# The front of an attention and feed-forward kernel, written out block by block

## The chip, the cores and the metric

The kernel runs on one core of one Trainium2 chip, in one launch. The metric is the device time in microseconds (us), taken as the median of several executions. One further execution was profiled, and all rows below are of that one.

## The reference

x is 2 x 2048 tokens of 256 numbers, in float32.

```python
xn = layernorm(x)                                  # no gain, no bias
q, k, v = split(xn @ w_qkv)                        # 16 heads of 16
q, k = irfft(rfft(q) * mask), irfft(rfft(k) * mask)   # along each head's 16; mask = sigmoid(logits)
attn = softmax(q @ k.T / 4) @ v @ w_out + b_out
h = square(relu(xn @ W_fc.T)); y = h @ W_proj.T
spikes = 5 steps of a leaky integrate-and-fire on y, averaged
out = x + attn + spikes
```

The filter on q and k is linear in a head's 16 numbers, so the kernel folds it into the weights.

## The kernel before

The five engines have instruction streams of their own, written by hand: PE (matmul), DVE, ACT, POOL and SP, which issues the DMAs. Semaphores order them. The change concerns the front, the work before the first softmax, and leaves the 32 passes (16 heads x 2 batches) and the end as they are.

The front handles the 4096 tokens in 8 blocks of 512. x_in holds two blocks of x, x_norm two normalised ones. For a block t:

- SP loads x (`load_x`), 512 KB.
- DVE `normalise`: statistics (4 instructions and 4 aggregations), five small instructions for the root with one square root on ACT (`deviation`), and scaling (4 instructions).
- PE `transpose_block`: 8 transposes into `even_slot`; ACT `take_transposed` copies them to xb, POOL from there to xnT.
- PE `project_qk`: four groups w = 0 to 3, two for Q and two for K, each of 2 matmuls (4 instructions in the trace), into two PSUM banks in turn. ACT `take_high` copies a group to the high part of the buffer hilo[w], DVE `low_parts` subtracts it from the group for the low part and frees the bank: group w waits for the low part of group w - 2.
- SP `store_block`: two stores of 256 KB per group, from hilo[w] to the scratch qk_scratch in DRAM. hilo[w] lies in probs (w = 0, 1), relu_sb (2) and hid_sb (3). ACT writes hilo[w] of the next block only when these stores have landed (semaphore stored[w]).
- PE `project_v`: 16 instructions into `odd_slot`; ACT `take_v` copies them out.

The order is: on PE Q/K(t), transposes(t+1), V(t); on DVE low parts(t), normalise(t+2); on SP the load of x(t+2), then the stores of t. Before block 0, DVE builds the filter, PE folds it into the weights in `odd_slot` (`fold_filter`), and ACT copies these out.

Heads need, per 128 queries, the maximum over all keys ahead of the exponentials. `first_max` computes 48 such pieces (128 queries x 512 keys) for head 0 in the front: one matmul on PE and one reduction on DVE each, with two places in PSUM. Its operands are the stack (`load_stack`), read back from the scratch at the start of block 4, once the stores of blocks 0 to 3 have landed. In blocks 5 to 7 the matmuls stand between those of Q/K (8 a block) and in blocks 6 and 7 also between those of V (8 a block); 8 more follow after block 7. `split_shift` on DVE turns the maxima of the first 1024 queries into rows of the stack, which SP writes (`store_shift`).

After the front PE computes scores, ACT takes exponentials into probs (all stores must have landed, as hilo[0] and hilo[1] lie there), and PE multiplies with V.

Of the kernel before, what the change touches and what calls it, by code (L numbers as in the profile page):

```python
# [17 lines left out]
P = 128  # L18
# [8 lines left out]
BLK = 512  # L27
# [14 lines left out]
AHEAD = [0, 4, 8, 8]  # L42
# [16 lines left out]
def build(nc, x, wqk, wv, wout, bout, logits, wfc, wproj, basis, eye, out):  # L59
    with ExitStack() as ctx:  # L60
# [44 lines left out]
        x_norm = attn[:, 2 * KT:4 * KT, :].rearrange("p (b k) d -> p b k d", b=2)  # L105
# [30 lines left out]

        def score_slot(g):
            return ring[:, (4 * (g // 2) + g % 2) % 3, :]
# [11 lines left out]
        const_in = sem("const_in")  # L150
        late_in = sem("late_in")
# [17 lines left out]
        stored = [sem(f"stored{i}") for i in range(QB)]  # L169
        v_ready = sem("v_ready")  # L170
        v_taken = sem("v_taken")
        stack_in = [sem(f"stack_in{i}") for i in range(2)]
# [50 lines left out]
        def _(sp):  # L223
# [17 lines left out]
            def store_block(t):  # L241

                for w in range(QB):
                    g = w % 2
                    sp.wait_ge(lo_done, QB * t + w + 1 + QK_BANKS)
                    for part in range(2):
                        dst = qk_dram[w // 2, g * 8:(g + 1) * 8, part, :, bass.ds(t * BLK, BLK)]
                        sp.dma_start(dst, hilo[w][:, part, :]).then_inc(stored[w], 16)  # L248
# [43 lines left out]
            for t in range(NB // 2, NB):  # L292
                if t < NB - 2:
                    next_x(t, t % 2)
                if t == NB // 2:
                    for w in range(QB):
                        sp.wait_ge(stored[w], 32 * (NB // 2 + 1))
                    sp.wait_ge(zero_out, 64)
                    load_stack(0, 0)
# [3 lines left out]
                store_block(t)  # L303

                if t == NB // 2:
                    sp.dma_start(wfc_sb[:], wfc.rearrange("(c p) e -> p c e", p=P)).then_inc(late_in, 16)
                if t == NB // 2 + 1:
                    sp.dma_start(wproj_sb[:], wproj.rearrange("(c p) e -> p c e", p=P)).then_inc(late_in, 16)
                if t == NB // 2 + 2:
                    sp.dma_start(wout_sb[:], wout.rearrange("(c p) e -> p c e", p=P)).then_inc(late_in, 16)  # L310
                    sp.dma_start(bout_sb[:], bout.partition_broadcast(P)).then_inc(late_in, 16)
            store_shift(0, 0, 0)
            for w in range(QB):
                sp.wait_ge(stored[w], 32 * (NB + 1))
# [47 lines left out]
        def _(pool):  # L362
# [18 lines left out]
            for w in range(QB):  # L381
                pool.sem_inc(stored[w], 32)
# [69 lines left out]
        def _(act):  # L452
# [14 lines left out]
            def take_high(t):  # L467
                for w in range(QB):
                    act.wait_ge(qk_ready, QB * t + w + 1)
                    act.wait_ge(stored[w], 32 * (t + 1))  # L470
                    act.activation(hilo[w][:, 0, :].bitcast(F32R), qk_psum(w), ACT.Copy).then_inc(hi_ready, 1)
# [7 lines left out]
            take_transposed(0, 0)  # L479

# [4 lines left out]
            with act.Fori(0, NB // 4) as n:  # L485
                for p in range(2):
                    t = 2 * n + p
                    take_high(t)
                    take_transposed(t + 1, 1 - p)
                    deviation(t + 2)  # L490
                    take_v(t)
            for t in range(NB // 2, NB):
                take_high(t)
                if t < NB - 1:
                    take_transposed(t + 1, (t + 1) % 2)
                if t < NB - 2:
                    deviation(t + 2)
                take_v(t)
# [27 lines left out]
            for w in range(QB):  # L526
                act.wait_ge(stored[w], 32 * (NB + 1))
# [20 lines left out]
        def _(pe):  # L548
            def transpose_block(t, p):
                pe.wait_ge(ln_done, t + 1)  # L550
                for c in range(KC):
                    for k in range(KT):
                        mm = pe.transpose(even_slot[:, c * BLK + k * P:c * BLK + (k + 1) * P],
                                          x_norm[:, p, k, c * P:(c + 1) * P], ident[:])
                mm.then_inc(tr_done, 1)

            def fold_filter():

                pe.wait_ge(const_in, 48)
                pe.wait_ge(filt_dve, NF + 2)  # L560
                for w in range(QB):
# [6 lines left out]
            def first_max(n):  # L568

                tile, chunk, c = n // 4, n % 4, n % 2  # L570
                pe.wait_ge(mx_taken, n + 1)
                pe.matmul(mx[:, c, :], qst[0][:, tile * P:(tile + 1) * P], kst[0][:, chunk * BLK:(chunk + 1) * BLK],
                          start=True, stop=True).then_inc(mx_ready, 1)
# [31 lines left out]
            transpose_block(0, 0)  # L605
            fold_filter()
            pe.wait_ge(fold_taken, 1)
            with pe.Fori(0, NB // 4) as n:
                for p in range(2):
                    t = 2 * n + p  # L610
                    project_qk(t, p)
                    next_transpose(t + 1, 1 - p)
                    project_v(t, p)

            chunk = 0
            for t in range(NB // 2, NB):
                units = AHEAD[t - NB // 2]
                if units and not chunk:
                    pe.wait_ge(stack_in[0], STACK)
                    pe.wait_ge(blank_in, 16)  # L620
                    pe.wait_ge(preset, 8)
                project_qk(t, t % 2, chunk if units else None)
                if t < NB - 1:
                    next_transpose(t + 1, (t + 1) % 2)
                project_v(t, t % 2, chunk + 2 * QB if units > QB else None)
                chunk += 2 * units
# [32 lines left out]
            def pair(h, b, s, last=False, beside=lambda: None):  # L659
# [7 lines left out]
                if s == LEAD and ahead:  # L667
                    pe.wait_ge(stack_in[mb], STACK * (h + 1 + b))
# [48 lines left out]
            def head(h, b, last=False):  # L717
                i = 2 * h + b

                def beside(s):  # L720
# [5 lines left out]
                    if s == 10:  # L726
                        pe.wait_ge(misc_taken, use(i, DOWN))
                        pe.wait_ge(squared, 2 * i + 3)
                        down(0)
# [31 lines left out]
            pe.wait_ge(late_in, 64)  # L761
# [42 lines left out]

            end_transpose(0, 0)
# [11 lines left out]
        def _(dve):  # L817
            LN_LINKS = 7

            def normalise(t, n, p):  # L820

                base = LN_LINKS * t
                dve.wait_ge(x_landed[p], 16 * (n + 1))
# [10 lines left out]
                dve.tensor_scalar(rstd[:, 0, :], meanvar[:, :, 1], EPS, None, ALU.add).then_inc(var_ready, 1)  # L834
                dve.wait_ge(std_ready, t + 1)
# [9 lines left out]
                dve.wait_ge(ln_step, base + 7)  # L845
                dve.wait_ge(tr_done, t + 1)
                for k in range(KT):
                    last = dve.tensor_scalar(x_norm[:, p, k, :], x_in[:, p, k, :], meanvar[:, k, 0:1],
                                             rstd[:, 4, k:k + 1], ALU.subtract, ALU.mult)
                last.then_inc(ln_done, 1)  # L850

# [17 lines left out]
            def first_max(n):  # L869
                tile, chunk = n // 4, n % 4  # L870
# [10 lines left out]
            def low_parts(t, n=None):  # L881
                for w in range(QB):
                    if n is not None:
                        for c in range(2):
                            first_max(n + 2 * w + c)
                    dve.wait_ge(hi_ready, QB * t + w + 1)
                    dve.tensor_tensor(hilo[w][:, 1, :].bitcast(F32R), qk_psum(w), hilo[w][:, 0, :],
                                      ALU.subtract).then_inc(lo_done, 1)
# [24 lines left out]
            normalise(0, 0, 0)  # L913
            build_filter()
            normalise(1, 0, 1)
            with dve.Fori(0, NB // 4) as n:
                for p in range(2):
                    t = 2 * n + p
                    low_parts(t)
                    normalise(t + 2, n + 1, p)  # L920
            chunk = 0
            for t in range(NB // 2, NB):
                units = AHEAD[t - NB // 2]
                low_parts(t, chunk if units else None)
                if t < NB - 2:
                    normalise(t + 2, t // 2 + 1, t % 2)
                if t == NB - 1:
                    for link in range(4):
                        split_shift(link, 0, 0, 2 * TB)
                if units > QB:  # L930
                    for n in range(chunk + 2 * QB, chunk + 2 * units):
                        first_max(n)
                chunk += 2 * units
            for n in range(chunk, 2 * (UNITS - LEAD)):
                first_max(n)
# [75 lines left out]
            dve.wait_ge(late_in, 64)  # L1011
# [56 lines left out]
```

## Time and profile before

| | us |
|---|---|
| median of 3 runs | 1870.12 |
| lowest, highest | 1869.64, 1870.3 |
| profiled execution | 1869.74 |
| its span, from first to last instruction | 1867.9 |
| PE busy | 1827.9 (98%) |
| DVE busy | 1400.3 (75%) |
| ACT busy | 1082.9 (58%) |
| POOL busy | 712.1 (38%) |

Busy times are sums over the span. PE's counts modelled ends of pipelined matmuls, so 98% does not mean that PE is at its peak. Times on the trace's clock run from the first instruction of the profiled execution.

### The profile page before, as it was taken

How to read it: one execution, taken by the hardware profiler on the slowest of the kernel's cores; microseconds unless marked ns; L12 is line 12 of the kernel's file. 1: busy time of each engine (PE TensorE's matmuls, PEld its weight loads, DVE VectorE, ACT ScalarE, POOL GpSimd, SP SyncE). 2: the span in 40 equal slices, each digit the busy share in tenths (PEclk: the TensorE clock that was granted, in tenths of full speed). 3: DMA queues.
4: the chain of work that ended last, by engine and by line, in shares of the span. 5: the costliest groups of instructions: out<-in, count | busy, mean ns of one | idle time of the engine just before them, and what ended most of it. 6: DMA issues, size and time to landing. Idle time of an engine off the chain costs nothing.

```text
span 1867.9 us, 35365 instructions
## 1 busy us (share of the span) xinstructions
PE 1827.9 (98%) x14352; PEld 1097.1 (59%) x14352; DVE 1400.3 (75%) x1724; ACT 1082.9 (58%) x1189; POOL 712.1 (38%) x948
## 2 busy tenths in 40 slices
PE   6889999999999999999999999999999999999998
PEld 4556555655555555555555555555555655555556
DVE  5576777777777777777777777777777777777737
ACT  3225666666666666666666666666666666656661
POOL 1000444443333444443333444443333444443344
PEclk9998999999999999999999999999999999999999
DMA  4751222121122222221122222221122222121105
GB/s 157 223 198 32 41 41 41 35 41 27 22 41 41 41 41 41 35 41 24 24 41 41 41 41 41 35 41 24 24 41 40 41 41 41 35 41 22 26 24 158
DMA packets 49083, 94.57 MB, mean 51 GB/s; under 512 B 13910, under 2 KB 27990, under 8 KB 44826
## 3 DMA queue, kind: packets, MB, share of 16 engines
q1 hardware_dynamic: 48924, 92.35, 22.5%
q8 instruction: 112, 1.84, 0.4%
q14 instruction: 47, 0.39, 0.1%
HBM read 70.80 MB, written 20.99 MB: 49 GB/s over the span
## 4 chain that ended last, share of the span: by engine, by line
PE 87%; DVE 7%; DMA 2%; SPq 1%; issue 1%; ACT 1%; ACTq 0%; DVEq 0%
PE ring L642 28%; PE banks L652 25%; PE ring L632 17%; PE banks L714 6%; PE banks L709 5%; DVE pmax L878 5%; DMA qk_scratch<-hid_sb 1%; PE banks L581 1%; PE ring L634 1%; SPq L248 1%; PE ring L800 1%; DVE attn L951 1%; ACT probs L503 1%; DMA attn<-x 1%; PE banks L800 1%
## 5 line engine op out<-in xcount | busy, mean ns | idle before, releaser
L878 DVE TENSOR_REDUCE pmax<-ring 128x2 f32<-128x1024 f32 x1000 | 1182.7, 1219 | 366.3 <-PE ring L634 363.2
L503 ACT ACTIVATE probs<-ring 128x1024 f32<-128x1024 f32 x1024 | 993.4, 1022 | 644.2 <-PE ring L642 644.2
L642 PE MATMUL ring<-qst,kst 66*128 66x512 f32 x2048 | 614.6, 421 | 2.4 <-ACT probs L503 1.3
L652 PE MATMUL banks<-probs,vst 128*32 128x256 f32 x8192 | 548.6, 385 | 0.1
L642 PEld LDWEIGHTS ring<-qst,kst 66*128 66x128 f32 x2048 | 345.3, 188 | 260.7 <-issue 206.1
L632 PE MATMUL ring<-kst,qst 64*128 64x512 f32 x1000 | 385.1, 465 | 3.6
L634 PE MATMUL ring<-kup,qup 64*128 64x512 f32 x1000 | 385.0, 465 | 0.0
L652 PEld LDWEIGHTS banks<-probs,vst 128*32 128x32 f32 x8192 | 213.8, 109 | 219.1 <-issue 130.5
L423 POOL TENSOR_TENSOR lif<-lif 128x256 f32<-128x256 f32 x32 | 19.6, 613 | 796.4 <-ACT y_sb L519 796.4
L632 PEld LDWEIGHTS ring<-kst,qst 64*128 64x128 f32 x1000 | 181.3, 183 | 161.5 <-DVE pmax L878 94.0
L634 PEld LDWEIGHTS ring<-kup,qup 64*128 64x128 f32 x1000 | 181.2, 183 | 0.0
L709 PEld LDWEIGHTS banks<-xnT,wfc_sb 128*128 128x128 f32 x1024 | 155.3, 192 | 22.5
L709 PE MATMUL banks<-xnT,wfc_sb 128*128 128x128 f32 x1024 | 156.7, 276 | 0.0
L714 PE MATMUL banks<-wproj_sb,hid_sb 128*128 128x256 f32 x512 | 152.4, 378 | 0.0
L411 POOL TENSOR_TENSOR hid_sb<-relu_sb 128x512 f32<-128x512 f32 x64 | 66.7, 1042 | 152.3 <-ACT relu_sb L508 152.3
L433 POOL TENSOR_SCALAR lif<-lif 128x256 f32<-128x256 f32 x128 | 110.4, 863 | 10.8
L434 POOL TENSOR_SCALAR lif<-lif 128x256 f32<-128x256 f32 x128 | 110.1, 860 | 8.0
L714 PEld LDWEIGHTS banks<-wproj_sb,hid_sb 128*128 128x128 f32 x512 | 96.7, 189 | 22.3
L432 POOL TENSOR_TENSOR lif<-lif 128x256 f32<-128x256 f32 x128 | 95.2, 744 | 10.0
L428 POOL TENSOR_TENSOR lif<-lif,y_sb 128x256 f32<-128x256 f32 x128 | 94.4, 738 | 10.7
L430 POOL TENSOR_TENSOR lif<-lif 128x256 f32<-128x256 f32 x128 | 94.3, 737 | 10.0
L581 PE MATMUL banks<-probs,counts 128*128 128x512 f32 x128 | 64.6, 629 | 7.6 <-DMA kst<-qk_scratch 5.7
(77 smaller groups left out, 685.5 us busy)
## 6 DMA issues: line engine op xcount, KB each, us to landing
qst<-qk_scratch SPq DMA_DIRECT2D x128, 128.0 KB, 4.1
kst<-qk_scratch SPq DMA_DIRECT2D x64, 256.0 KB, 6.0
qup<-qk_scratch SPq DMA_DIRECT2D x252, 64.0 KB, 5.0
qk_scratch<-probs SPq DMA_DIRECT2D x32, 256.0 KB
kup<-qk_scratch SPq DMA_DIRECT2D x64, 128.0 KB, 6.4
attn<-x SPq DMA_DIRECT2D x8, 512.0 KB, 7.6
qk_scratch<-relu_sb SPq DMA_DIRECT2D x16, 256.0 KB
qk_scratch<-hid_sb SPq DMA_DIRECT2D x16, 256.0 KB
```

The costliest lines, as they stand in the source:

```text
L428: pool.tensor_tensor(upd, decayed, y_sb[:], ALU.add).then_inc(lif_step, 1)
L432: pool.tensor_tensor(acc, acc, spks[(step + 1) % 2], ALU.add).then_inc(lif_step, 1)
L433: pool.tensor_scalar(spks[step % 2], mem, 1.0, None, ALU.is_gt)
L434: pool.tensor_scalar(decayed, mem, BETA, None, ALU.mult).then_inc(lif_step, 1)
L503: act.activation(probs[:, s % PS, :], score_slot(g), ACT.Exp, scale=SCALE).then_inc(exp_done, 1)
L632: pe.matmul(slot[:, 0:BLK], qst[b][0:SIDE, toks], kst[b][0:SIDE, 2 * part * BLK:(2 * part + 1) * BLK], start=True, stop=True)
L634: pe.matmul(slot[:, BLK:2 * BLK], qup[SIDE:2 * SIDE, toks], kup[b][SIDE:2 * SIDE, part * BLK:(part + 1) * BLK], start=True, stop=True).the ...
L642: mm = pe.matmul(score_slot(g)[:, c * BLK:(c + 1) * BLK], kst[b][:, kt * P:(kt + 1) * P], qst[b][:, q:q + BLK], start=True, stop=True)
L652: mm = pe.matmul(po[32 * j:32 * (j + 1), half * D:(half + 1) * D], vst[b][:, kt, :], quarters[:, j], start=(kt == 0), stop=(kt == TB - 1))
L709: mm = pe.matmul(misc[:, (f % 4) * P:(f % 4 + 1) * P], wfc_sb[:, c, f * P:(f + 1) * P], xnT[:, c, tile * P:(tile + 1) * P], start=(c == 0) ...
L714: return pe.matmul(misc[:, 0:D], hid_sb[:, f, :], wproj_sb[:, f, :], start=(f == 0), stop=(f == FC - 1))
L878: dve.tensor_reduce(pmax[:, tile, first:first + 2], unit_slot(g).rearrange("p (c e) -> p c e", c=2), AX, ALU.max).then_inc(mx_taken, 1)
```

## The change

- `normalise` is cut into statistics, root and scaling. From block 1 on, they are done for block t+3 between the low parts of block t: statistics after low part 0, root after 1, scaling after 2. In block 0 they are done for block 2 there, and for block 3 after the block. x_norm holds three blocks.
- x(t+4) is loaded behind the stores of block t.
- V of block 0 is computed before the filter is folded.
- The stack is loaded in two pieces, of 1024 tokens each, behind the stores of blocks 2 and 4.
- The 48 first maxima stand in V of blocks 4 to 6 and in Q/K of blocks 5 to 7, 8 in each, and their order follows the pieces (`first_part`).
- wfc is loaded behind the stores of block 5, with a semaphore of its own; wproj, wout and bout behind the last stores.
- stored[w] becomes two semaphores, for odd and even blocks, and the loops over blocks are written out.

Its core, cut:

```diff
+PIECE = 6 * 16
-        x_norm = attn[:, 2 * KT:4 * KT, :].rearrange("p (b k) d -> p b k d", b=2)
+        x_norm = [attn[:, (2 + i) * KT:(3 + i) * KT, :] for i in range(3)]
+        def first_part(n):
+            if n < 2 * TB:
+                return n % TB // 2, n // TB * 2 + n % 2
+            return n // 4, n % 4
...
@@ SP @@
-            def next_x(t, p):
-                sp.wait_ge(ln_done, t + 1)
-                load_x(t + 2, p)
+            def next_x(t):
+                sp.wait_ge(ln_done, t - 1)
+                load_x(t, t % 2)
+            def load_first(piece):
+                for w in range(QB):
+                    for k in range(2):
+                        sp.wait_ge(stored[w][k], 32 * (piece + 1))
+                cols = slice(piece * HALF, (piece + 1) * HALF)
+                for part in range(2):
+                    for dup in range(2):
+                        r = (2 * part + dup) * DH
+                        sp.dma_start(qst[0][r:r + DH, cols].bitcast(F32), qk_dram[0, 0, part, :, cols]).then_inc(first_in, 16)
+                for dup in range(2):
+                    r = dup * 2 * DH
+                    sp.dma_start(kst[0][r:r + 2 * DH, cols].bitcast(F32),
+                                 qk_dram[1, 0, :, :, cols].rearrange("r d t -> (r d) t")).then_inc(first_in, 16)
-            with sp.Fori(0, NB // 4) as n:
-                for p in range(2):
-                    next_x(2 * n + p, p)
-                    store_block(2 * n + p)
...
+            next_x(2)
+            next_x(3)
+            for t in range(NB):
+                store_block(t)
+                if t + 4 < NB:
+                    next_x(t + 4)
+                if t == 2:
+                    sp.wait_ge(zero_out, 64)
+                    sp.dma_start(qst[0][4 * DH:ROWS, :].bitcast(F32), zero_dram).then_inc(blank_in, 16)
+                    load_first(0)
+                if t == 4:
+                    load_first(1)
                     load_upper_keys(0, 0)
                     load_upper_queries(0, 0, 1)
+                if t == 5:
+                    sp.dma_start(wfc_sb[:], wfc.rearrange("(c p) e -> p c e", p=P)).then_inc(wfc_in, 16)
+                if t == 6:
+                    store_shift(0, 0, 0)
+            sp.dma_start(wproj_sb[:], wproj.rearrange("(c p) e -> p c e", p=P)).then_inc(wproj_in, 16)
@@ ACT @@
             deviation(0)
             take_transposed(0, 0)
+            take_v(0)
             act.wait_ge(fold_done, 1)
...
+            for t in range(NB):
+                for w in range(QB):
+                    take_high(t, w)
+                    if w == 1 and t == 0:
+                        deviation(2)
+                    if w == 1 and 0 < t < NB - 3:
+                        deviation(t + 3)
                 if t < NB - 1:
                     take_transposed(t + 1, (t + 1) % 2)
+                if t == 0:
+                    deviation(3)
+                else:
+                    take_v(t)
@@ PE @@
             transpose_block(0, 0)
+            pe.wait_ge(const_in, 48)
+            pe.wait_ge(xb_ready, 1)
+            project_v(0, 0)
             fold_filter()
             pe.wait_ge(fold_taken, 1)
+            for t in range(NB):
+                project_qk(t, t % 2, TB * (t - 5) + 8 if t > 4 else None)
                 if t < NB - 1:
                     next_transpose(t + 1, (t + 1) % 2)
+                if t:
+                    project_v(t, t % 2, TB * (t - 4) if 3 < t < NB - 1 else None)
...
-            for n in range(chunk, 2 * (UNITS - LEAD)):
-                first_max(n)
@@ DVE @@
+            normalise(0)
             build_filter()
+            normalise(1)
+            for t in range(NB):
+                ahead = t + 3 if t else 2
+                for w in range(QB):
+                    if t > 4:
+                        for n in range(2):
+                            first_max(TB * (t - 5) + 8 + 2 * w + n)
+                    low_part(t, w)
+                    if ahead < NB:
+                        if w == 0:
+                            block_stats(ahead)
+                        if w == 1:
+                            block_rstd(ahead)
+                        if w == 2:
+                            block_scale(ahead)
+                if t == 0:
+                    normalise(3)
+                if t == 6:
                     for link in range(4):
                         split_shift(link, 0, 0, 2 * TB)
+                if 3 < t < NB - 1:
+                    for n in range(8):
+                        first_max(TB * (t - 4) + n)
```

The matching waits follow: PE waits for `first_in` before maxima 0 and 16, for wfc_in before the first up-projection and for wproj_in before the first down-projection.

## Rows read from the trace of the kernel before

**Rows 1.** Busy time by stretch: span, busy us (instructions) of each engine, granted clock, DMA share, GB/s.

```profile
42.90:54.10 11.20, 11.20 (x41) 6.78 (x41) 6.20 (x19) 4.33 (x6) 1.04 (x1) 1.00 0.59 214
77.30:98.90 21.60, 15.66 (x50) 9.37 (x50) 10.23 (x24) 4.42 (x7) 0.97 (x1) 0.84 0.79 226
...
120.10:141.00 20.90, 19.22 (x57) 10.76 (x56) 18.71 (x33) 4.38 (x6) 0.40 (x1) 0.93 0.52 155
```

**Rows 2.** Chain of waits in order of time: start us, us, what.

```profile
20.12 7.18 PE banks L581 x16
...
28.18 3.46 PE ring L593 x16
...
53.30 9.27 DMA qk_scratch<-hid_sb
...
87.44 12.55 DMA attn<-x
...
108.29 1.71 PE banks L581 x2
...
114.02 0.88 PE ring L553 x8
...
120.24 0.86 PE banks L581 x2
...
128.75 0.25 PE ring L572
```

**Rows 3.** Timeline of SP's queue: issue start us, us of issuing, what, count.

```profile
52.50 1.43 SPq L248 DMA_DIRECT2D qk_scratch<-hid_sb  x2
54.14 0.51 SPq L225 DMA_DIRECT2D attn<-x  x1
...
123.78 3.44 SPq L248 DMA_DIRECT2D qk_scratch<-probs  x4
...
137.33 1.73 SPq L255 DMA_DIRECT2D qst<-qk_scratch  x4
```

**Rows 4.** DMA issues from 54 to 55 us: KB, us to landing.

```profile
attn<-x SPq DMA_DIRECT2D x1, 512.0 KB, 9.8
```

**Rows 5.** DMA issues from 9 to 10 us, the load of block 2.

```profile
attn<-x SPq DMA_DIRECT2D x1, 512.0 KB, 4.0
```

**Rows 6.** Timeline of ACT and PE: start us, us, instruction, [idle before <- releaser].

```profile
11.65 1.02 ACT L464 ACTIVATE probs<-ring 128x1024 f32<-128x1024 f32 x1 [4.55 <-PE ring L553]
...
14.96 3.75 PE L563 MATMUL ring<-counts 128*128 128x128 f32 x16 [3.35 <-DVE counts L866]
...
18.75 1.02 ACT L482 ACTIVATE counts<-ring 128x1024 f32<-128x1024 f32 x1 [6.08 <-PE ring L563]
...
60.09 0.60 ACT L471 ACTIVATE relu_sb<-banks 128x512 fp32r<-128x512 f32 x1 [1.91 <-DMA qk_scratch<-relu_sb]
...
62.66 0.60 ACT L471 ACTIVATE hid_sb<-banks 128x512 fp32r<-128x512 f32 x1 [1.97 <-DMA qk_scratch<-hid_sb]
...
105.36 0.80 PE L572 MATMUL ring<-kst,qst 66*128 66x512 f32 x1 [3.47 <-DVE pmax L872]
...
142.27 1.28 ACT L503 ACT_TABLE_LOAD   x1 [5.93 <-PE ring L642]
...
152.42 1.19 PE L642 MATMUL ring<-qst,kst 66*128 66x512 f32 x4
```

**Rows 7.** Groups of DVE by form up to 141.2 us: busy us, mean ns, idle before.

```profile
L872 DVE TENSOR_REDUCE pmax<-ring 128x1 f32<-128x512 f32 x47 | 31.4, 687 | 11.9 <-PE ring L572 11.9
...
L825 DVE BATCH_NORM_STATS2 stats<-attn 128x6 f32<-128x256 f32 x32 | 11.2, 413 | 6.3 <-DMA attn<-x 6.3
L848 DVE TENSOR_SCALAR attn<-attn,meanvar,rstd 128x256 f32<-128x256 f32 x32 | 11.0, 409 | 0.3
L887 DVE TENSOR_TENSOR probs<-banks,probs 128x512 fp32r<-128x512 f32 x16 | 11.0, 688 | 7.3 <-ACT probs L471 7.3
...
L831 DVE BATCH_NORM_AGGREGATE meanvar<-stats 128x2 f32<-128x6 f32 x32 | 3.0, 156 | 0.3
```

More of the change, by code:

```diff
@@ L41 @@
 QK_BANKS = 2
-AHEAD = [0, 4, 8, 8]
+PIECE = 6 * 16
 USES = 3
@@ L168, in build @@
         lo_done = sem("lo_done")
-        stored = [sem(f"stored{i}") for i in range(QB)]
+        stored = [[sem(f"stored{i}_{k}") for k in range(2)] for i in range(QB)]
         v_ready = sem("v_ready")
         v_taken = sem("v_taken")
+        first_in = sem("first_in")
         stack_in = [sem(f"stack_in{i}") for i in range(2)]
@@ L302, in _ @@
                     load_upper_queries(0, 0, 1)
[L303 to L311, printed above, removed]
@@ L312, in _ @@
-            store_shift(0, 0, 0)
+                if t == 5:
[3 more added lines that the diff above has]
+            sp.dma_start(wproj_sb[:], wproj.rearrange("(c p) e -> p c e", p=P)).then_inc(wproj_in, 16)
+            sp.dma_start(wout_sb[:], wout.rearrange("(c p) e -> p c e", p=P)).then_inc(late_in, 16)
+            sp.dma_start(bout_sb[:], bout.partition_broadcast(P)).then_inc(late_in, 16)
@@ L313, in _ @@
             for w in range(QB):
-                sp.wait_ge(stored[w], 32 * (NB + 1))
+                for k in range(2):
+                    sp.wait_ge(stored[w][k], 32 * (NB // 2))
             def head(h, b, last=False):
@@ L465, in take_transposed, with take_high @@
                                ACT.Copy).then_inc(xb_ready, 1)
[L467 to L471, printed above, removed]
+            def take_high(t, w):
+                act.wait_ge(qk_ready, QB * t + w + 1)
+                if t:
+                    act.wait_ge(stored[w][(t - 1) % 2], 32 * ((t - 1) // 2 + 1))
+                act.activation(hilo[w][:, 0, :].bitcast(F32R), qk_psum(w), ACT.Copy).then_inc(hi_ready, 1)
             def take_v(t):
@@ L526, in _ @@
             for w in range(QB):
-                act.wait_ge(stored[w], 32 * (NB + 1))
+                for k in range(2):
+                    act.wait_ge(stored[w][k], 32 * (NB // 2))
             for s in range(FIRST):
@@ L605, in _ @@
             transpose_block(0, 0)
+            pe.wait_ge(const_in, 48)
+            pe.wait_ge(xb_ready, 1)
+            project_v(0, 0)
             fold_filter()
             pe.wait_ge(fold_taken, 1)
[L608 to L622, printed above, removed]
+            for t in range(NB):
+                project_qk(t, t % 2, TB * (t - 5) + 8 if t > 4 else None)
                 if t < NB - 1:
                     next_transpose(t + 1, (t + 1) % 2)
-                project_v(t, t % 2, chunk + 2 * QB if units > QB else None)
-                chunk += 2 * units
+                if t:
+                    project_v(t, t % 2, TB * (t - 4) if 3 < t < NB - 1 else None)
             def maxima(g, unit, b):
@@ L844, in normalise, with block_scale @@
                 dve.tensor_tensor(rstd[:, 4, :], rstd[:, 3, :], rstd[:, 2, :], ALU.mult).then_inc(ln_step, 1)
[L845 to L846 removed]
+            def block_scale(t):
+                dve.wait_ge(ln_step, LN_LINKS * t + 7)
+                if t > 2:
+                    dve.wait_ge(tr_done, t)
                 for k in range(KT):
[L848 removed]
+                    last = dve.tensor_scalar(x_norm[t % 3][:, k, :], x_in[:, t % 2, k, :], meanvar[:, k, 0:1],
                                              rstd[:, 4, k:k + 1], ALU.subtract, ALU.mult)
                 last.then_inc(ln_done, 1)
+            def normalise(t):
+                block_stats(t)
+                block_rstd(t)
+                block_scale(t)
             def build_filter():
@@ L879, in unit_max, with low_part @@
                                   unit_slot(g).rearrange("p (c e) -> p c e", c=2), AX, ALU.max).then_inc(mx_taken, 1)
[L881 to L888, printed above, removed]
+            def low_part(t, w):
+                dve.wait_ge(hi_ready, QB * t + w + 1)
+                dve.tensor_tensor(hilo[w][:, 1, :].bitcast(F32R), qk_psum(w), hilo[w][:, 0, :],
+                                  ALU.subtract).then_inc(lo_done, 1)
             def split_shift(link, n, half, chunks=None):
```

76 lines of the change are left out of this document (23 added, 53 removed).

## The prediction

> **What bounds the kernel now.** I began with the table of stretches [rows 1]. Of the 1867.9 us span, the front (normalisation, projections, first maxima) takes 141 us, to the end of the last stretch; the first exponential starts at 143.55 us, after its table load [rows 6]. From there on no instruction changes, so the forecast is the shift of that first exponential, less what the following pairs win back. PE is busy without pause in block 2 (the row from 42.9 stands for three like it), then idles 5.9 us in block 4's stretch, at a mean granted clock of 0.84 [rows 1], and 3.47 us ahead of block 6's maxima [rows 6]; DVE is busy 55% of block 2 and 90% of the last stretch [rows 1].
>
> Second, the chain of waits [rows 2]. In blocks 1 to 3 much of it runs not over PE but over the last stores of a block: a hid_sb store takes 9.27 us from issue to landing, because it queues behind the others. ACT waits for relu_sb's store until 60.09 and for hid_sb's until 62.66 us [rows 6]: a pair of stores (high and low part) drains in 2.57 us. Later in the chain the x of block 7 takes 12.55 us [rows 2]. PE alone would need, per block, 6.9 us of Q and K (16 instructions at 0.43, half of the 0.86 per two), 0.88 of transposes and 3.46 of V: 11.25 us [rows 2].
>
> Third, where x stands in this queue. Block 5's load is issued at 54.14 us, just behind the last store of block 2 [rows 3], and takes 9.8 us to land [rows 4]: at 63.9, some 1.3 us after the last of those stores (62.6 [rows 6]). So x lands behind every store issued before it, and adds some 1.4 us of its own. Four pairs and one x make 4 x 2.57 + 1.4 = 11.7 us. The block 2 load, with nothing in front, landed in 4.0 us [rows 5]. In the kernel before the wait is harmless, as statistics come after all four low parts of the next block.
>
> **The change, part by part.** I add everything on the trace's own clock.
>
> *Start.* V of block 0 moves into the time in which PE waits for the filter. Its input is ready at 11.65 + 1.02 = 12.7 us; the filter fold began at 14.96 [rows 6]. V costs 3.46 us at 2.4 GHz [rows 2] and twice that, 6.9, at 1.2 GHz (a pair of Q/K instructions took 1.71 us at half clock, 0.86 at full [rows 2]). PE has just run 8 transposes, so I take 4.5 us. Then the copy out, 1.02 plus 0.4 of handing over, because the fold writes the same bank; then the fold, 3.75 us before [rows 6] and half of it, 1.9, if V has brought the clock up; then the copy of the weights and its handing over, 1.4 (18.71 to 20.12 [rows 6, 2]). Q and K of block 0 start at 12.7 + 4.5 + 1.4 + 1.9 + 1.4 = 21.9 us instead of 20.12; bounds 20.9 (V at full clock) and 26.1 (both at half). The 3.46 us of V saved later are PE time only.
>
> *Statistics moved between the low parts.* DVE now runs, inside the four Q/K groups of block t: low part 0, statistics of block t+3 (4 x 0.41 + 0.6 of aggregation = 2.0 us), low part 1, the root chain (1.0), low part 2, scaling (4 x 0.41), low part 3 [rows 7]. With two banks, PE's group 3 waits for low part 1, so a late statistic stops PE, ACT (the next high part) and SP (the next stores). If x is there this costs little: 0.9 us a block, a period of 12.1 instead of 11.25 or 11.7.
>
> *But x(t+3) is late.* SP issues it behind all eight stores of block t-1, and statistics want it right after low part 0 of block t. Block 0: low parts end about 25.4, 28.2, 29.8 and 31.9. Four pairs take 13.5 us from first issue to last landing when the queue starts empty (123.78 to 137.33 [rows 3]); x(3) now lies ahead of them (1.4) and x(4) behind (1.4). X(4), the landing of x(4), is 25.5 + 13.5 + 2.8 = 41.8 us. Block 1's low part 0 stands behind all of block 3's normalisation: 31.9 + 2.0 + 1.2 + 1.4 + 0.7 = 37.2. So DVE waits 4.6 us, and PE about 5, long enough for half clock (a 3.47 us gap at 101.9 was followed by 1.71 us pairs [rows 6, 2]).
>
> From then on each x gates the next. From X: statistics 2.0, low part 1 0.69, handing over 0.1, the issue at X + 2.8; three pairs from a queue that has run dry, 13.5 - 2.57 = 10.9; x 1.4. The period is 15.1 us. PE would be ready earlier: group 3 to X + 4.6, transposes, V to X + 9, low part 0 of the next block X + 12.3; it waits some 2 us each time. Lower bound 12.1 (nothing late), upper 16.5 (each of the three pairs and x 0.35 us slower, if the queue has to start up anew). I take 15.1, because each term is a measured one. X(7) = 41.8 + 3 x 15.1 = 87.1 us.
>
> *A rule against the rows.* The x load is 512 KB; by rows it lands after 9.8 us behind stores and 4.0 us alone [rows 4, 5]. The Trainium skill, "DMA: Bandwidth & Descriptors", section "Anatomy of one DMA", gives about 2.0 us fixed plus bytes over 436 GB/s (for the GpSimd path), so some 3.2 us here, an estimate from that page. By it x would land before it is wanted, and the shift would be that of rival 1. The trace disagrees for a full queue and is near it for an empty one.
>
> *First stack in two pieces.* load_first(0) puts 6 reads of half the size and the blank behind x(6), ahead of block 3's stores: about 3 us of queue, in the part of the cycle in which the queue runs dry; nothing, if that holds, and about 3.4 more if each half-size read costs as much as a whole one. The 5.7 us wait for the whole stack at block 4, and the late x(7) behind the 1 MB of wfc (12.55 us [rows 2]), are gone: that is the gain. wproj, wout and bout come after the last store and wproj, the first wanted, is read some 20 us after the first exponential; its own 1 MB and the second batch's stack (wanted 16 us after it, 11 us to load) fit. Loops written out, two semaphores for each store buffer and the other counts change no duration that these rows show; if their cover were short, it would be by tenths.
>
> *Maxima from block 4 on.* The same 48: 8 in V of blocks 4 to 6, 8 in Q/K of 5 to 7. Each costs PE 0.23 us [rows 2] and DVE 0.69 or less [rows 7]. So Q/K with maxima is 8.75 us (120.24 to 129.0), V with 8 is 5.34 (114.90 to 120.24), transposes 0.88 [rows 2]: 14.97 us a block. DVE needs 8 x 0.67 in V, just fits. The tail of maxima after the last V (6 us, DVE-bound, at half clock) goes.
>
> *Sum.* Q/K of block 5 starts at X(7) + 2.8 + 0.1 + 1.7 (group 3) + 0.88 + 5.34 + 0.3 = 98.2 us. The end of Q/K 7 is 98.2 + 2 x 14.97 + 8.75 = 136.9. V 7 ends 140.4, scores may start at 141.8, near the 141.0 of before (the end of the last stretch [rows 1]). But the exponentials also wait for the last stores, as probs shares their buffers. Before, these landed 8.4 us after Q/K 7 (128.9 to 137.3 [rows 2, 3]), covered by V and the tail of maxima. Now that cover is V alone: 136.9 + 8.4 = 145.3, plus 1.28 of table load: first exponential at 146.6 us, 3.0 later than 143.55. Before, the third pair's scores came 8.9 us after it (152.42 [rows 6]), partly at half clock; now the scores are already there, but a PE gap of some 3 us will lower the clock again: I credit 0.7 (bounds 0 and 2.4). Shift: +2.3 us. The profiled execution took 1869.74 us, 1.84 over its span, and the median is 1870.12; so I predict 1870.12 + 2.3 = 1872.4 us. Measurement can tell about 0.2%, 3.7 us.
>
> **The rivals.**
> 1. x is in time (faster). Should loads overtake stores (the DMA share in block 2 was 0.59, so there is room [rows 1]), the period is 12.1: block 1's group 3 needs no wait, Q/K 2 starts at 46 us, Q/K 5 at 46 + 2 x 12.1 + 14.5 (block 4 with 8 maxima) = 84.8, 13 us earlier than the 98.2: a shift of about -11, 1859 us; with x late by half as much, 1865. For it: 4.0 us on an empty queue. Against: the 9.8 us row, and 12.55 for x(7). Chance 0.2. The Trainium skill's 3.2 us ("DMA: Bandwidth & Descriptors", "Anatomy of one DMA") is one way into this rival, at the same 1859 us, and I give it 0.05 on its own.
> 2. The reads of the first piece collide (slower). If load_first(0) costs a whole stack's time, or store pairs restart at 3 us spacing, X(7) is 3.4 later and all behind it: +5.7, 1875.8 us. It decides from about 1.5 us of extra in the three cycles together. For it: the queue is then full at 73 us when block 3's stores come. Against: half the bytes. Chance 0.25.
> 3. The last stores don't bind, since the queue is less loaded at the end: the scores then start at 141.8 and all of it comes out at 1870 to 1871 us. Chance 0.1.
> The main case keeps 0.45, with a range of its own of 1869.5 to 1875.
>
> **How the numbers follow.** Faster by over 0.2% is rival 1, 0.2. Slower is rival 2 and the upper edge of the main case, 0.25 + 0.07. The same is the rest of the main case and rival 3, 0.38 + 0.1. The range takes the main case, rival 3, most of rival 2 (its two causes together would pass 1877) and the milder half of rival 1: 1863.5 to 1877.
>
> **What would show it.** In the profile after: DVE's statistics in blocks 1 to 4 idle before them, released by attn<-x; x landing about 1.4 us after the stores ahead of it; blocks 1 to 4 spaced about 15 us, blocks 5 to 7 about 15.0; Q/K 0 starting at 21.9; ACT's first exponential released by a store's landing at about 145.3. The prediction is wrong if statistics find x there, if the spacing is 12, or if the first exponential is released by PE.

## The result: slower, 1879.2 us against 1869.9

The changed kernel takes 1879.2 us (median of 6), the kernel before 1869.88 in the same measurement: a ratio of 1.0050, 95% interval 1.0037 to 1.0063. I had forecast 1872.4, within 1863.5 to 1877. The profiled span is 1877.5 us, 9.6 more than before.

The chain of waits of the changed kernel shows the mechanism that I had described, in four copies (start us, us, what):

```profile
12.78 6.54 PE ring L618 x16
...
37.11 6.92 DMA attn<-x
44.06 1.41 DVE stats L840 x4
...
53.16 6.77 DMA attn<-x
59.95 1.41 DVE stats L840 x4
...
68.52 9.47 DMA attn<-x
78.01 1.41 DVE stats L840 x4
...
87.22 6.56 DMA attn<-x
93.81 1.41 DVE stats L840 x4
...
145.64 6.87 DMA qk_scratch<-hid_sb
```

The loads of blocks 4 to 7 are in the chain, each with the statistics behind it; in the kernel before only that of block 7 was. Their landings, 44.0, 59.9, 78.0 and 93.8 us, are 15.9, 18.1 and 15.8 us apart. The timeline of the same kernel tells who was held:

```profile
12.78 6.53 PE L618 MATMUL ring<-counts,probs 128*128 128x256 f32 x16 [1.16 <-issue]
...
20.51 2.02 PE L583 MATMUL ring<-counts 128*128 128x128 f32 x16 [1.21 <-ACT v_all L494]
...
23.65 5.44 PE L606 MATMUL banks<-probs,counts 128*128 128x512 f32 x12 [1.11 <-ACT counts L502]
...
44.06 1.41 DVE L840 BATCH_NORM_STATS2 stats<-attn 128x6 f32<-128x256 f32 x4 [5.88 <-DMA attn<-x]
...
46.73 3.78 PE L606 MATMUL banks<-probs,counts 128*128 128x512 f32 x4 [6.52 <-DVE probs L909]
...
62.62 1.98 PE L606 MATMUL banks<-probs,counts 128*128 128x512 f32 x4 [1.52 <-DVE probs L909]
...
78.01 1.41 DVE L840 BATCH_NORM_STATS2 stats<-attn 128x6 f32<-128x256 f32 x4 [6.00 <-DMA attn<-x]
...
80.69 3.78 PE L606 MATMUL banks<-probs,counts 128*128 128x512 f32 x4 [6.60 <-DVE probs L909]
...
152.75 1.28 ACT L522 ACT_TABLE_LOAD   x1 [4.56 <-DMA qk_scratch<-hid_sb]
154.04 1.94 ACT L522 ACTIVATE probs<-ring 128x1024 f32<-128x1024 f32 x2
155.12 0.79 PE L647 MATMUL ring<-kst,qst 64*128 64x512 f32 x1 [4.36 <-ACT probs L522]
...
162.36 1.19 PE L657 MATMUL ring<-qst,kst 66*128 66x512 f32 x4
```

PE's last Q/K group waits for DVE's low part, which stands behind the statistics, which wait for x. The gaps of 6.5 us are followed by a group at half clock (3.78 us), the one of 1.52 us by a group at full clock (1.98 us). Once x no longer gates, from 104.5 us on, blocks 5 and 6 take 15.0 and 15.3 us. The table by stretch has block 3 first, for comparison (21.0 us, mean granted clock 0.76), then blocks 5 and 6:

```profile
68.80:89.80 21.00, 14.40 (x41) 8.46 (x40) 6.56 (x23) 4.53 (x7) 1.04 (x1) 0.76 0.63 177
...
104.50:119.50 15.00, 15.00 (x58) 9.79 (x57) 13.04 (x21) 4.47 (x7) 1.04 (x1) 1.00 0.67 190
119.50:134.80 15.30, 15.25 (x58) 9.73 (x57) 13.50 (x25) 4.45 (x7) 1.04 (x1) 1.00 0.63 231
```

What the change was to win is there: neither the 5.7 us wait for the stack nor the tail of maxima comes back, and PE is busy for all but 0.05 us of these two stretches, where in the kernel before it idled 5.9 us in block 4's and 1.7 us in the last one [rows 1]. The first exponential starts at 154.04 instead of 143.55 us, the third pair's scores at 162.36 instead of 152.42 [rows 6]: 9.9 us later; the span has grown by 9.6, so what follows takes as long as before.

### The profile page after: what moved, and what is told of

Read it like the earlier page. It is cut to its first block, busy times and chain, and to the rows that moved or that the text cites. A ratio compares the mean times of both kernels' runs of the same rounds, so it can differ in the third digit from the quotient of the medians.

```text
span 1877.5 us, 35174 instructions
## 1 busy us (share of the span) xinstructions
PE 1825.1 (97%) x14352; PEld 1095.6 (58%) x14352; DVE 1399.6 (75%) x1724; ACT 1083.1 (58%) x1189; POOL 711.6 (38%) x948
## 4 chain that ended last, share of the span: by engine, by line
PE 87%; DVE 8%; DMA 2%; issue 1%; ACT 1%; SPq 0%; ACTq 0%; DVEq 0%
PE ring L657 28%; PE banks L667 24%; PE ring L647 17%; PE banks L729 5%; PE banks L724 5%; DVE pmax L904 5%; DMA attn<-x 2%; PE banks L606 2%; PE ring L649 1%; PE ring L618 1%; ACT probs L522 1%; PE ring L814 1%; DVE attn L975 1%; PE ring L597 1%; PE banks L814 1%
## 5 line engine op out<-in xcount | busy, mean ns | idle before, releaser
L452 POOL TENSOR_SCALAR lif<-lif 128x256 f32<-128x256 f32 x128 | 109.6, 856 | 10.8
L447 POOL TENSOR_TENSOR lif<-lif,y_sb 128x256 f32<-128x256 f32 x128 | 94.5, 738 | 10.7
```

The lines of the kernel that those rows point to most:

```text
L452: pool.tensor_scalar(spks[step % 2], mem, 1.0, None, ALU.is_gt)
```

## The experiments

All are timed against the kernel before, whose median was 1869.9 to 1871.9 us in these comparisons. Differences below 2 us between two rows, and those between ratios whose intervals overlap, are therefore not shown by the medians alone; where I lean on one, the traces are named.

| kernel | median us | ratio to before, 95% interval |
|---|---|---|
| changed kernel | 1879.20 | 1.0050 (1.0037 to 1.0063) |
| x_early | 1865.87 | 0.9974 (0.9965 to 0.9983) |
| stats_after | 1868.37 | 0.9986 (0.9978 to 0.9995) |
| v_back | 1876.03 | 1.0032 (1.0020 to 1.0044) |
| reads_later | 1876.72 | 1.0031 (1.0019 to 1.0043) |
| v_only | 1870.66 | 1.0000 (0.9991 to 1.0009) |
| exp_split | 1880.96 | 1.0055 (1.0043 to 1.0067) |
| split_w | 1873.56 | 1.0014 (1.0005 to 1.0023) |
| x_early_split | 1859.77 | 0.9938 (0.9924 to 0.9952) |
| all_v_back | 1859.48 | 0.9934 (0.9920 to 0.9949) |
| all_stats | 1865.42 | 0.9965 (0.9952 to 0.9977) |

**x_early: the load one block sooner.**

```diff
+            def store_block(t, between=None):
...
+                    if w == 3 and between is not None:
+                        between()
...
-                store_block(t)
+                store_block(t, (lambda: next_x(4)) if t == 0 else None)
-                if t + 4 < NB:
-                    next_x(t + 4)
+                if t + 5 < NB:
+                    next_x(t + 5)
```

So x(4) is issued ahead of the last pair of block 0, and x(5) to x(7) one block sooner. The two stack pieces also get a semaphore each, here and in stats_after, reads_later and the combined kernels.

> The changed kernel with one edit in SP's order: x(t+4) is issued behind the stores of block t-1 instead of block t, so a whole block earlier (x(4) ahead of the last stores of block 0). The two stack pieces land on two semaphores. Theory (each x lands 1.3 us behind the stores queued ahead of it, and statistics between the low parts pass that wait to PE and to the next stores): DVE's statistics of blocks 5 to 7 find x there, block 4's wait falls from 5.9 to about 2.5 us, blocks are spaced about 12 us instead of 16 to 18, Q/K of block 5 starts near 88 instead of 104.7 us, and the time falls by 10 to 17 us, to 1862 to 1869. Rival (the queue's throughput or the order on DVE itself sets the spacing, not the landing): the spacing stays at 14 us or more, and the time at 1874 or above.

1865.87 us, 13.3 less than the changed kernel and 0.26% less than the one before. DVE's wait in block 1 is halved, and the later statistics wait for nothing:

```profile
39.60 1.41 DVE L842 BATCH_NORM_STATS2 stats<-attn 128x6 f32<-128x256 f32 x4 [2.89 <-DMA attn<-x]
53.27 1.40 DVE L842 BATCH_NORM_STATS2 stats<-attn 128x6 f32<-128x256 f32 x4
65.24 1.07 DVE L842 BATCH_NORM_STATS2 stats<-attn 128x6 f32<-128x256 f32 x3
```

The statistics of the last three blocks (53.3, 65.2 and, not shown, 77.2 us) are 12.0 us apart, the period that I had worked out for DVE and PE alone (12.1). The place of four loads in SP's order was moved, and beside the split semaphore nothing else, so the late landing of x is shown to be the cause, and the rival falls. The profiled execution, at 1862.6 us, lies 3.3 below the median, and its first Q/K starts at 22.2 instead of 23.7 us, before any edited load matters: of the 4.5 us by which x(4)'s statistics are earlier, 1.5 are that.

**stats_after: the statistics out of x's way instead.**

```diff
                     low_part(t, w)
-                    if ahead < NB:
+                    if t == 0:
                         if w == 0:
                             block_stats(ahead)
...
-                if t == 0:
-                    normalise(3)
+                if t + 3 < NB:
+                    normalise(t + 3)
```

> The changed kernel with the statistics, root and scaling of block t+3 moved behind all four low parts of block t (blocks 1 to 4), on DVE and on ACT; x is still issued behind the stores of block t. The two stack pieces land on two semaphores. Theory (x is late, but harmless if only the normalisation waits for it): x lands as late after its issue as in the changed kernel, yet PE's group 3 no longer waits; blocks are spaced 11.7 to 12.5 us, Q/K of block 5 starts near 87, and the time falls by 10 to 18 us, to 1861 to 1869. Rival (what costs is x's late issue itself or the load on the queue): the wait only moves to the transposes and the time stays within 3 us of 1879.

1868.37 us, 10.8 less, with x issued as late as in the changed kernel. So the late load costs only where something urgent stands behind its reader. It stays behind x_early. A cause that the trace shows is that in block 4 the normalisation now stands ahead of the first maxima, and PE waits 5.0 us for their reduction:

```profile
83.34 1.39 DVE L838 BATCH_NORM_STATS2 stats<-attn 128x6 f32<-128x256 f32 x4
...
87.93 1.28 DVE L896 TENSOR_REDUCE pmax<-ring 128x1 f32<-128x512 f32 x2
...
88.67 0.79 PE L595 MATMUL ring<-kst,qst 66*128 66x512 f32 x1 [4.97 <-DVE pmax L896]
```

**v_back: V of block 0 where it was.**

```diff
-            project_v(0, 0)
             fold_filter()
...
-                if t:
+                if t >= 0:
                     project_v(t, t % 2, ...)
```

> The changed kernel with V of block 0 back behind the transposes of block 1, as in the kernel before. Theory (the front is a chain from the first store through the landings of x; PE has slack in it, and V ahead of the filter, 6.5 us at half clock, only delays its start): Q/K of block 0 starts at 20.1 instead of 23.65, x(4) lands near 40.5 instead of 44.0, and the time falls by about 3.5 us, to 1875.7. Rival (PE's own work sets the front, so that hiding V behind the filter is worth its 3.5 us): the time stays or rises by up to 3 us.

1876.03 us, 3.2 less, near the 3.5 expected; the two intervals (1.0020 to 1.0044 and 1.0037 to 1.0063) overlap, so the size is uncertain. The trace has the mechanism, but less of it reaches the end: Q/K 0 starts 3.8 us earlier (19.8), x(7) lands 2.6 earlier, and the first exponential stands at 153.26, 0.8 earlier. Part of the lead goes in block 4, where a gap of 2.95 us is followed by a slower group (2.90 us, in the changed kernel 1.98):

```profile
84.21 6.96 DMA attn<-x
...
93.87 2.90 PE banks L603 x4
```

V hidden in the filter's wait is thus rather a loss here: it delays the first store, from which the chain runs, and saves PE time that PE does not lack.

**v_only: the same part alone, in the kernel before** (its four looped blocks written out on PE and ACT).

```diff
             transpose_block(0, 0)
+            project_v(0, 0)
             fold_filter()
...
-                    project_v(t, p)
+                if t:
+                    project_v(t, t % 2)
```

> The kernel before with one part of the change alone: V of block 0 ahead of the filter fold. Theory (6.5 us of V at half clock delay the first Q/K and the first store by 3.5 us; the front of the kernel before is a chain of stores in blocks 1 to 3, which this delays, and PE's saved 3.5 us only shorten a wait in it): the first Q/K at 23.6 instead of 20.1 us, and the time rises by 0 to 3.5 us, to 1870.8 to 1874.3, likeliest 1872.5. Rival (PE's work is the limit, so that V in the filter's gap is worth up to 3.5 us): the time falls by 1 us or more.

1870.66 us, a ratio of 1.0000 (0.9991 to 1.0009). The first Q/K starts 3.8 us later and the first exponential, in its profile, at 146.02, 2.5 us later, but the medians differ by 0.3. The interval excludes a change of over 1.7 us either way, and with it the rise of 2.2 us that I had held likeliest. A rise of 1 us is as open as the rival's fall of 1: alone, this part is worth nothing that can be measured.

**reads_later: the first stack piece behind block 3's first stores.**

```diff
+                    if t == 3 and w == 1:
+                        load_first(0)
                     sp.wait_ge(lo_done, QB * t + w + 1 + QK_BANKS)
...
                 if t == 2:
-                    load_first(0)
```

> The changed kernel with the six reads of the first stack piece issued behind block 3's first pair of stores instead of right behind x(6); the two pieces land on two semaphores. Theory (the 18.1 us between the landings of x(5) and x(6), against 15.9 and 15.8 in the two other cycles, come from these reads running beside x(6): it landed 3.4 us after the stores ahead of it, all others 1.3): x(6) lands 1.3 us behind its stores, that cycle falls to 16 us, and the time by about 2 us, to 1877. Rival (the second store of the last pair, issued 1.2 us late, made that cycle long, or the reads cost the same wherever they stand): the sum of the two cycles around them stays at 33.9 us and the time at 1879.2, within 0.7.

1876.72 us, 2.5 less (intervals 1.0019 to 1.0043 and 1.0037 to 1.0063, which overlap; the trace decides). The chain of this kernel has the third load at the length of the others:

```profile
52.74 6.70 DMA attn<-x
...
68.44 7.09 DMA attn<-x
...
84.82 6.73 DMA attn<-x
```

The load of block 6 takes 7.09 us instead of 9.47, and the cycle that it ends 16.1 instead of 18.1. That is 2.0 of the 2.5 us; Q/K 0 also starts 0.5 us earlier in this profile (23.18), which the edit does not touch. So reads issued behind a load do hold it up; my expectation that they fill an idle queue looked only at what stands behind them.

**exp_split: the first exponential freed from the last stores.**

```diff
-            for w in range(QB):
-                for k in range(2):
-                    act.wait_ge(stored[w][k], 32 * (NB // 2))
             for s in range(FIRST):
+                if s == 2:
+                    for w in range(2):
+                        for k in range(2):
+                            act.wait_ge(stored[w][k], 32 * (NB // 2))
...
+                    for k in range(2):
+                        act.wait_ge(stored[2][k], 32 * (NB // 2))
```

The second of the added waits is at s == 4, and POOL waits for stored[3] ahead of its first square.

> The changed kernel, with the wait of the first exponential for the last stores cut in parts: the exponentials into probs 2 and 3 wait for the stores of hilo 0 and 1 (issued first), relu_sb's writer and hid_sb's writer each for their own. Theory (the last store, landing 8.8 us after the last Q/K, is what holds the first exponential at 154.0 us and opens the 4.4 us gap on PE): the first exponential starts near 150.7, released by PE, PE stays at full clock, and the time falls by 3 to 5 us, to 1874 to 1876. Rival (this stretch is limited by PE or won back by the following pairs): within 1 us of 1879.2.

A miss: 1880.96 us, 1.8 above the changed kernel; in ratios 1.0055 against 1.0050, so no difference. The exponential did come early, and then PE stopped elsewhere:

```profile
149.32 1.94 ACT L524 ACTIVATE probs<-ring 128x1024 f32<-128x1024 f32 x2
...
151.62 1.72 SPq L264 DMA_DIRECT2D qst<-qk_scratch  x4
...
167.59 2.05 PE L662 MATMUL ring<-qst,kst 66*128 66x512 f32 x4 [5.58 <-DMA qup<-qk_scratch]
168.82 1.94 ACT L524 ACTIVATE probs<-ring 128x1024 f32<-128x1024 f32 x2 [7.44 <-PE ring L662]
```

The fifth pair needs the stack of the second batch, whose reads are issued when the last store has landed (151.62). It was the next limit, and close: in the changed kernel the fifth pair stands at 169.31. The lead of 1.7 us that exp_split has there goes in the slower pair behind the gap (2.05 us instead of 1.2).

**split_w: the weights ahead of the last block.** On top of exp_split:

```diff
                 if t == 6:
                     store_shift(0, 0, 0)
+                    sp.dma_start(wproj_sb[:], ...)
+                    sp.dma_start(wout_sb[:], ...)
+                    sp.dma_start(bout_sb[:], ...)
...
-            sp.dma_start(wproj_sb[:], ...)
-            sp.dma_start(wout_sb[:], ...)
-            sp.dma_start(bout_sb[:], ...)
```

> exp_split with a second edit: wproj, wout and bout are loaded behind the stores of block 6 instead of behind the last stores. In exp_split the first exponential came 4.7 us earlier, but PE then waited 5.6 us at the fifth pair for qup of the second stack, which landed 14.7 us after its first issue (11.1 in the kernel before, where these weights were loaded earlier). Theory (the second stack, behind the last store, is the next limit, and the 1.4 MB of weights ahead of it make it 3.5 us later): that wait falls from 5.6 to 2 us or less and stays at full clock, and the time falls by 5 to 7 us, to 1872 to 1874.5. Rival (the loads are bound by the last store alone, the weights cost nothing): the wait stays at 5 us and the time at 1879 to 1881.

1873.56 us, 7.4 less than exp_split and 5.6 less than the changed kernel. The first exponential is where exp_split had it, and the wait has shrunk:

```profile
150.00 1.94 ACT L524 ACTIVATE probs<-ring 128x1024 f32<-128x1024 f32 x2
...
164.03 1.16 PE L662 MATMUL ring<-qst,kst 66*128 66x512 f32 x4 [1.32 <-DMA qup<-qk_scratch]
```

So two waits had stood one behind the other, both on the last store, and the change had put 1.4 MB of weights into the second. The weights moved without the split exponential were not run.

**x_early_split: these edits and x_early.**

```diff
-                store_block(t)
-                if t + 4 < NB:
-                    next_x(t + 4)
+                store_block(t, (lambda: next_x(4)) if t == 0 else None)
+                if t + 5 < NB:
+                    next_x(t + 5)
```

> All edits of x_early, exp_split and split_w together. Theory (they remove different waits, one between the blocks and one at the end of the front): their gains add up, 13 us and 5 to 7 us, to 1858 to 1862 us, with the first exponential near 133. Rival (the gains are the same time counted twice): 1865 or 1866, as x_early alone.

1859.77 us, 0.62% less than the kernel before (0.48 to 0.76). 13.3 and 5.6 us were gained apart, 19.4 together: the gains add up.

**all_v_back: the same with V of block 0 back.**

```diff
-            project_v(0, 0)
             fold_filter()
...
-                if t:
+                if t >= 0:
                     project_v(t, t % 2, ...)
```

> x_early_split with V of block 0 back behind the transposes of block 1, as in v_back. Theory (with x early, blocks from 2 on are spaced 12 us by DVE and PE, and only block 1 still waits, 3.3 us in DVE, for x(4)): the stores of block 0 and x(4) come some 3 us earlier and block 1's wait nearly goes, while Q/K of block 1 starts where it did, behind V; the time falls by 1 to 3 us, to 1857 to 1859. Rival (with x no longer gating, V in the filter's gap is at last worth its PE time): the time rises by 1 to 3 us, to 1861 to 1863.

1859.48 us: no difference, as neither theory had it. The expected shift in the blocks came (Q/K of block 5 starts at 85.5 instead of 90.0 us), but the reads of the second stack now hold the fifth pair by 2.01 us instead of 1.03, and it runs slower (1.88 us instead of 1.17):

```profile
146.10 1.88 PE L659 MATMUL ring<-qst,kst 66*128 66x512 f32 x4 [2.01 <-DMA qup<-qk_scratch]
```

In x_early_split the fifth pair starts at 149.56, 3.5 us later. Behind it the granted clock is 0.50 (150 to 155 us; 1.00 in x_early_split), and the seventh pair starts at 157.13 against 156.07: in these two profiles what the front wins is lost at that limit and in the slow pairs behind it. The six runs spread over 1856.4 to 1864.2 us, and the profiled one took 1861.1, so whether the faster ones keep some of the gain stays open.

**all_stats: the same as x_early_split with stats_after.**

```diff
-                    if ahead < NB:
+                    if t == 0:
                         if w == 0:
                             block_stats(ahead)
...
+                if t + 3 < NB:
+                    normalise(t + 3)
```

> x_early_split with the normalisation of block t+3 behind the low parts of block t (blocks 1 to 4), as in stats_after. Theory (normalisation between the low parts costs 0.9 us a block once x is there, but behind them it stands, in block 4, ahead of the first maxima, where it held PE for 5.0 us in stats_after): Q/K starts of blocks 2 to 4 are spaced 11.3 to 11.7 us instead of 12.0 and Q/K 2 starts 3 to 4 us earlier, and block 4 loses about 5 us; the time is 1857 to 1861, no better than 1859.8 by more than 2.5 us. Rival (the order on DVE is what costs): it falls by 4 us or more, to 1855 or below.

1865.42 us, slower than either theory had it. Block 4 takes 25.3 us from Q/K start to Q/K start (70.6 to 95.9), of which I had allowed 20. The normalisation of block 7 ends at 88.4, the reductions of all 8 maxima of V come behind it, and PE waits 6.0 us for the first. The low part ahead of the normalisation is late too, as it waits for a hid_sb store that takes 10.5 us to land:

```profile
83.71 1.39 DVE L845 BATCH_NORM_STATS2 stats<-attn 128x6 f32<-128x256 f32 x4
...
87.00 1.38 DVE L874 TENSOR_SCALAR attn<-attn,meanvar,rstd 128x256 f32<-128x256 f32 x4
88.30 1.28 DVE L903 TENSOR_REDUCE pmax<-ring 128x1 f32<-128x512 f32 x2
```

Normalisation between the low parts, the change's own order, is thus the better one once x is early.

## Why the prediction was wrong

The step that failed is the cycle from one x to the next: forecast at 15.1 us, it took 15.9, 18.1 and 15.8. Most of the rest of the miss is a start that was 1.8 us later. The mechanism held, in its order: the statistics of blocks 4 to 7 were released by x, the spacing fell to 15 us behind them, the first exponential was released by the last store. The sizes did not, nearly all in the same direction, and the sum left the range.

| term of the sum | predicted us | measured us |
|---|---|---|
| V of block 0 | 4.5 | 6.53 |
| start of Q/K 0 | 21.9 | 23.65 |
| landing of x(4) | 41.8 | 44.0 |
| three cycles to x(7) | 45.3 (3 x 15.1) | 49.8 (15.9 + 18.1 + 15.8) |
| x(7) to start of Q/K 5 | 11.1 | 10.7 |
| Q/K 5 to end of Q/K 7 | 38.7 | 39.2 |
| to the last landing | 8.4 | 8.8 |
| to the first exponential | 1.3 | 1.5 |
| first exponential | 146.6 | 154.04 |
| won back to the third pair | 0.7 | 0.5 |
| shift of the pairs behind | 2.3 | 9.9 |

- *Start.* I took 4.5 us for V, between 3.46 at full clock and 6.9 at half, and it ran at half rate but for its last few instructions; that the fold behind it would run at full rate was right (2.02 us instead of 3.75). Worth 1.8 us.
- *The cycle*, 4.5 us of the 7.4 by which the first exponential is off. The term "three pairs from a queue that has run dry, 10.9" was mis-sized: in the cycles without reads the path from the issue behind low part 1 to the landing of x took 13.2 us (46.7 to 59.9) instead of 12.3. The Q/K group at half clock does not explain it: in reads_later the cycle from x(5) to x(6) (59.4 to 75.5 us) lasted 16.1 us, with its group at full clock (1.98 us at 62.13). The view by stretches of 1 us of the changed kernel (last three columns: granted clock, DMA share, GB/s) shows that the queue does run dry and starts slowly:

```profile
44.00:45.00 1.00, 0.00 (x0) 0.00 (x0) 0.94 (x3) 0.00 (x0) 0.00 (x0) 0.50 0.51 197
46.00:47.00 1.00, 0.27 (x1) 0.27 (x2) 0.93 (x5) 0.69 (x2) 0.00 (x0) 0.50 0.02 6
48.00:49.00 1.00, 1.00 (x2) 0.41 (x2) 1.00 (x4) 0.00 (x0) 0.00 (x0) 0.50 0.50 51
51.00:52.00 1.00, 1.00 (x6) 1.00 (x5) 0.69 (x1) 0.15 (x1) 0.00 (x0) 0.50 0.52 178
```

After the dry spell the stores move some 10% slower than the 204 GB/s that they had in the kernel before with the same share. Why is open. The upper bound that I had set, 16.5, would have covered the cycles without reads, which makes some 2.4 of the 4.5 us; the other 2.1 are the reads.
- *The reads of the first piece.* My second rival: they cost 2.0 us of their cycle, 2.5 of the median (reads_later). Its other cause, slower store pairs, came too, by less. I had written that both together would pass 1877, and left that out of the range; that is what happened. But the term was "nothing, if they fall where the queue runs dry"; what I had not asked is what they do to the load ahead of them.
- *Rival 1*, x in time, is what x_early made true: its 12.1 us period is confirmed at 12.0. It had Q/K 5 at 84.8 us (its terms add up to 84.7); in x_early Q/K 5 starts at 88.9, 15.6 ahead of the changed kernel's 104.5. The rule of the Trainium skill, "DMA: Bandwidth & Descriptors", section "Anatomy of one DMA" (2.0 us and bytes over 436 GB/s, for the GpSimd path), does not hold for these loads from SP: 6.6 to 9.5 us, each behind stores.
- *The end.* The last store's landing held the exponential as forecast. But I had called the second stack covered ("wanted 16 us after, 11 us to load"); in exp_split it took some 16 us from the first issue until PE went on (151.6 to 167.6; the 14.7 in my expectation for split_w is too low), behind the weights that the change had moved there. That cost all that the earlier exponential could gain.
- *The range.* Its terms were bounded one by one, but I took the middle or the lower side of each. Three of them (half clock, the restart of the queue, the reads) depend on the same thing, a queue and an engine that come out of a gap, and went the same way; that they are one cause is argued, not shown. If they are, the chance of 0.32 for slower was too small for the same reason.

## What to carry to other kernels

When a step is moved ahead of urgent work in an in-order stream, ask first what its input waits for; an operand that arrives "in time" at the end of a block is late in its middle. Here the same reordering gained 0.26% instead of losing 0.5% when the load moved one block with it. And when a wait is removed, look for the next one on the same event: the last store released two waits, and the edit of the first alone was worth nothing, that of both 5.6 us.

## What was not expected of the hardware

- A load was held by DMAs issued behind it: with six small reads right behind x(6) it took 9.5 us, with them behind the next stores 7.1 (reads_later). The Trainium skill, "DMA: Bandwidth & Descriptors", section "Queues, rings and completion order", says that each DMA engine takes its descriptors in ring order, that a later one may finish its write before an earlier one, and that only the semaphore's increment waits for the earlier writes of its engine. That x lands behind all stores ahead of it (63.9 against 62.6 us in the kernel before) agrees; that later reads delay it is not in the rule, and on which DMA engine the 2.4 us arise no run here shows.
- While only stores of 256 KB move, the DMA share stays near 0.5 (0.47 to 0.53 from 49 to 55 us of the changed kernel). The Trainium skill, "DMA: Bandwidth & Descriptors", section "Rules for kernel authors", has the slowest dimension of the access pattern limit the engines used; the stores' is 8 heads, so 8 engines of 16, and the share agrees. Whether stores with a slowest dimension of 16 would shorten the front was not tried.
- The 16 V instructions of block 0, behind a pause of 1.2 us, took 6.53 us, all but the last few at half rate, where the 16 of the kernel before took 3.46, though the granted clock (first of the last three columns) shows full speed for this stretch:

```profile
12.80:19.30 6.50, 6.50 (x16) 4.93 (x16) 3.79 (x14) 0.00 (x0) 1.05 (x1) 1.00 0.02 6
```
